# Attention over sorted edges: the running block sum kept in two PSUM banks, copied out by ScalarE at each step, in place of a VectorE add

## The chip, the cores and the metric

The kernel runs on one core of one Trainium2 chip. The metric is the device time of one execution in microseconds (us), as the median of several runs of the same program. All inputs and outputs lie in the chip's memory (HBM).

## The reference

A graph of 6250 nodes (256 values each) and 100000 edges (`src`, `dst`; sorted by `dst`). Two layers are computed, each added to its input: an attention layer with 8 heads of 32 values, then a layer of messages in hyperbolic space. The change touches the attention layer alone:

```
h = relu(layernorm(x));  q, k, v = h @ W + b        # 6250 x 8 x 32 each
scores = sum(q[src] * k[dst]) / sqrt(32)            # 100000 x 8
m = segment_max(scores, dst);  e = exp(scores - m[dst])
z = segment_sum(e, dst);       p = e / max(z[dst], 1e-16)
x = x + segment_sum(v[src] * p, dst)
```

## The kernel before

A first stage sorts the edges for both layers and computes q, k and v. Then comes attention (`attention`), a middle stage, the messages (`messages`) and a last stage. They follow one another and share no work around this change.

In attention the nodes stand in 50 blocks (`NB`) of 127 rows. `acc_l0` in SBUF holds for each block 128 partitions (a node each) x 264 values (`AW`: 8 heads x (32 values and the sum of weights)). The sorted edges go through in 440 steps (`SUPER`) of two groups (`SPAN`) of 128 edges; all edges of a step have their `dst` in one block, whose offset in `acc_l0` is read from a table (`off`) into a register (`Starts.fetch`, L1819, and `Starts.values`, L1822). Four steps (`SG`) make a turn, two turns a window (8 steps, 55 windows). The softmax is taken as a running one: at each window a factor `fac` rescales the block that is being summed.

The code is unrolled: 110 turns, on each engine a function `period(t)` that takes its part of several turns at once (a software pipeline; `old` is four turns back, `ready` three). The engines meet by semaphores alone, and each works strictly in the order that `period` writes.

- TensorE: for each step p of `old`, `sums(old, p)`: two float32 matmuls of the one-hot rows `hot` with the weighted values `pv` into one of two PSUM banks, `out[:, p % 2]` (L2066; each shows as two records); then `near`, two matmuls that pick the keys of a later turn's edges into `kx` (L2046); then in some steps a piece of `chain`, small matmuls for the window's softmax maxima (L2078, L2083, L2087, and L2091 with L2093, which release ScalarE's weights). In a turn's first step `sums` waits for the one-hot rows (`hot_in`), the weights' sums (`z_in`) and the weighed values (`weighed`).
- VectorE: `mult` (L2217), `score` (L2228), `weigh` (L2196), the scans for the maxima (L2247 to L2285), once a window `rescale` (L2206: block times `fac`), and once a step `add` (L2238): block in `acc_l0` = block x `keep` + `out`, where `keep` is 1 if the step before had the same block and else 0. TensorE may refill a bank when its `add` is done (`summed`).
- ScalarE, in a turn: `hot_columns(t+1)` (L2124 after the DMA of marks has landed, L2126), once a window `weights` (L2147, L2150, after TensorE's L2093), `hot_rows(ready)` (eight of L2136, then L2139, which gives `hot_in`), `weight_sums(ready)` (L2158, which gives `z_in`).
- GpSimd gathers the rows of q and v by indirect DMA (L2020); SyncE issues the marks' DMA (L1982) when the second turn back has its keys (`kx_in`).

Of the kernel before, what the change touches and what calls it, by code (L numbers as in the profile page):

```python
# [9 lines left out]
I32 = mybir.dt.int32  # L10
# [1799 lines left out]
class Starts:  # L1810
# [10 lines left out]
    def values(self, first, n):  # L1821
        return [self.eng.snap(r, min_val=0, max_val=self.top) for r in self.regs[first:first + n]]  # L1822
# [66 lines left out]
def attention(nc, m, edges):  # L1889
# [17 lines left out]
    with Stage(nc, "at") as ctx:  # L1907
# [16 lines left out]
        blk, keep = rest[:, 0:1 + SUPER], m.tab_c[:, 2 * SLOT + 2 * G * P + G * DIM:][:, 0:SUPER]  # L1924
# [13 lines left out]
        out = pb("out", [P, 2, 512])  # L1938
# [6 lines left out]
        (c_in, made, hotT_in, hot_in, z_in, kx_in, mixed, scored, weighed, out_in, summed, t1_in, ran, ended, m1_in, carried, m2_in,  # L1945
         came_in, topped, cleared, readied, taken, t2_in, m3_in, far_rows, far_cols, p_in, fac_in, rescaled) = (sem(n) for n in (
             "c_in", "made", "hotT_in", "hot_in", "z_in", "kx_in", "mixed", "scored", "weighed", "out_in", "summed", "t1_in", "ran",
             "ended", "m1_in", "carried", "m2_in", "came_in", "topped", "cleared", "readied", "taken", "t2_in", "m3_in", "far_rows",
             "far_cols", "p_in", "fac_in", "rescaled"))

# [16 lines left out]
        with nc.Block() as block:  # L1967
# [58 lines left out]
            def _(pe):  # L2026
                TE = nc.tensor
                pe.wait_ge(c_in, 32)
                pe.wait_ge(made, 7)
                starts = Starts(pe, "at_pe", off, (NB - 1) * AW, 2)  # L2030

# [18 lines left out]
                def sums(t, p):  # L2050
# [9 lines left out]
                    if p >= 2:  # L2060
                        pe.wait_ge(summed, t.n * SG + p - 1)
                    elif t.plus(-1).exists():
                        pe.wait_ge(summed, t.plus(-1).n * SG + p + 3)
                    for k in range(SPAN):
                        j = SPAN * p + k
                        last = TE.matmul(out[:, p % 2, 0:AW], hot[:, t.h % 2, j, :], pv[:, t.h % 2, j].rearrange("p h d -> p (h d)"),  # L2066
                                         start=(k == 0), stop=(k == SPAN - 1))
# [47 lines left out]
            def _(act):  # L2115
# [3 lines left out]
                def hot_columns(t):  # L2119
# [4 lines left out]
                    A.activation(hotT[:, t.h % 2, :], hotT[:, t.h % 2, :], ACT.Abs, bias=m.minus_lane[:, 0:1]).then_inc(far_cols, 1)  # L2124
                    act.wait_ge(far_cols, t.n + 1)
                    A.activation(hotT[:, t.h % 2, :], hotT[:, t.h % 2, :], ACT.Relu, scale=-1.0, bias=one).then_inc(hotT_in, 1)  # L2126

                def hot_rows(t):
# [3 lines left out]
                    act.wait_ge(col_in[t.h], (t.i + 1) * 16)  # L2132
                    if t.plus(-2).exists():
                        act.wait_ge(out_in, t.plus(-2).n * SG + SG)
                    for k in range(G):
# [5 lines left out]
                def weights(w):  # L2141
# [6 lines left out]
                    if w.plus(-WG).exists():  # L2148
                        act.wait_ge(summed, w.plus(-WG).n * SG + 1)
# [746 lines left out]
```

## Time and profile before

| | |
|---|---|
| median of 3 runs | 3706.06 us (3704.23 to 3707.38) |
| span of the profiled execution | 4137.2 us, 55464 instructions (no time beside the span is given for it) |
| busy in it | PE 73%, PE weight load 58%, DVE 82%, ACT 53%, POOL 48% |
| mean granted TensorE clock | 0.889 of full speed |
| attention in it | from about 764 to 2150 us |

The profiled execution is 431 us longer than the median of the runs that carried no profiler. Engines are called PE, DVE, ACT, POOL and SP in the rows; a trailing q is that engine's sequencer (it issues, waits and loads registers, and is not counted as busy). In a timeline row the numbers are start and duration in us; the brackets hold the time that the engine stood idle before it, and what ended that.

### The profile page before, as it was taken

The page shows a single profiled execution, that of the slowest core. Times are in us where ns is not written, and L with a number is a line of the kernel's source. Part 1 is how long each engine was busy: PE and PEld are TensorE (multiplying, and loading weights), DVE is VectorE, ACT ScalarE, POOL GpSimd, SP SyncE. Part 2 cuts the span into 40 slices and gives each one's busy share as a digit, 9 for nine tenths or more (in the row PEclk, how much of TensorE's full clock was granted, in tenths as well). Part 3 has the DMA queues.
Part 4 walks back from the last instruction along what each step waited for, and adds up shares of the span by engine and source line. Part 5 has one row for each costly group of instructions (what it writes and reads, how often), then busy time and mean ns, then how long its engine had stood idle before and what let it go on. Part 6 is the DMA issues. An engine that isn't in the chain of part 4 may idle for free. (4 is left out here: it accounts for less than half of the span.)

```text
span 4137.2 us, 55464 instructions
## 1 busy us (share of the span) xinstructions
PE 3002.7 (73%) x12662; PEld 2413.6 (58%) x12662; DVE 3401.4 (82%) x9121; ACT 2194.8 (53%) x5961; POOL 1969.1 (48%) x2404
## 2 busy tenths in 40 slices
PE   3545444577777777677756688988988888888866
PEld 2434333455555555555545567777777777777754
DVE  8999996687888888788878378888888888888877
ACT  3235542444444444444438466666665666666557
POOL 1000003556666666666620366666666666666400
PEclk9867777788998889888988899999999999999988
DMA  2111004666667666666636655655655666556361
GB/s 65 39 55 38 13 26 148 191 202 208 202 208 216 207 209 208 211 205 209 206 98 174 172 161 168 173 163 168 171 168 167 167 172 170 166 167 170 89 145 50
DMA packets 295230, 635.60 MB, mean 154 GB/s; under 512 B 78197, under 2 KB 147123, under 8 KB 294657
## 3 DMA queue, kind: packets, MB, share of 16 engines
q0 software_dynamic: 141312, 463.96, 38.3%
q1 hardware_dynamic: 153602, 168.11, 14.5%
q8 instruction: 116, 1.90, 0.2%
q14 instruction: 200, 1.63, 0.1%
HBM read 587.26 MB, written 44.65 MB: 153 GB/s over the span
## 5 line engine op out<-in xcount | busy, mean ns | idle before, releaser
L2469 POOL DMA_INDIRECT area<-d_xr,col x880 | 890.2, 1012 | 686.8 <-DVE area L2706 236.8
L2562 PE MATMUL ms_near_a<-low,ms_hotT 128*128 x1760 | 550.4, 395 | 204.3 <-issue 99.2
L2066 PE MATMUL at_out<-at_pv,at_hot 128*128 128x264 f32 x1760 | 558.6, 447 | 75.7 <-issue 32.0
L2020 POOL DMA_INDIRECT low<-d_qv,col x440 | 449.6, 1022 | 265.6 <-DVE at_pv L2196 129.1
L2563 PE MATMUL ms_near_c<-tab_c,ms_hotT 128*128 x1760 | 536.1, 387 | 0.0
L2046 PE MATMUL at_kx<-area,tab_c 128*128 x1760 | 508.8, 417 | 21.8 <-issue 20.7
L2562 PEld LDWEIGHTS ms_near_a<-low,ms_hotT 128*128 128x128 f32 x1760 | 327.6, 192 | 301.6 <-issue 258.9
L2066 PEld LDWEIGHTS at_out<-at_pv,at_hot 128*128 128x128 f32 x1760 | 358.9, 217 | 161.9 <-issue 63.1
L2046 PEld LDWEIGHTS at_kx<-area,tab_c 128*128 128x128 f32 x1760 | 372.9, 213 | 96.0 <-issue 25.3
L2238 DVE SCALAR_TENSOR_TENSOR area<-area,tab_c,at_out 128x264 f32 x440 | 211.7, 481 | 216.4 <-remote 114.9
L2604 ACT COPY area<-area 128x2 f32<-128x2 f32 x440 | 82.0, 186 | 566.0 <-DVE area L2675 379.0
L2582 PE MATMUL ms_out<-ms_more,ms_hot 128*128 128x257 f32 x1408 | 369.0, 386 | 4.3 <-DVE low L2717 4.3
L2020 POOL DMA_INDIRECT tab_c<-d_qv,col x288 | 294.9, 1024 | 161.6 <-issue 87.2
L2563 PEld LDWEIGHTS ms_near_c<-tab_c,ms_hotT 128*128 128x128 f32 x1760 | 341.0, 194 | 51.6
L2706 DVE CUSTOM_DVE_ANT_0 area<-area 128x256 f32<-128x256 f32 x880 | 342.4, 426 | 23.5 <-issue 12.7
L2672 DVE TENSOR_TENSOR ms_more<-area,ms_near_a 128x514 f32<-128x514 f32 x352 | 239.0, 679 | 140.1 <-PE ms_near_c L2565 73.7
L2124 ACT ACTIVATE tab_c<-tab_c,minus_lane 128x1024 f32<-128x1024 f32 x110 | 126.2, 1147 | 417.8 <-DMA tab_c<-by_dst_marks 374.1
L2582 PEld LDWEIGHTS ms_out<-ms_more,ms_hot 128*128 128x128 f32 x1408 | 272.1, 194 | 47.1 <-ACT ms_more L2640 3.2
L2629 ACT ACTIVATE ms_junk<-ms_more 128x255 bf16<-128x255 f32 x704 | 282.2, 402 | 9.1 <-issue 0.4
L2696 DVE TENSOR_SCALAR ms_hot<-ramp,col,area 128x128 f32<-128x128 f32 x880 | 273.7, 353 | 1.8 <-PE ms_out L2582 1.6
L2136 ACT ACTIVATE at_hot<-ramp,col 128x128 f32<-128x128 f32 x880 | 267.8, 390 | 5.3 <-remote 5.3
L2565 PE MATMUL ms_near_c<-area,ident 128*128 128x256 f32 x880 | 269.1, 388 | 0.0
(375 smaller groups left out, 6560.6 us busy)
## 6 DMA issues: line engine op xcount, KB each, us to landing
tab_c<-by_dst_marks SPq DMA_DIRECT2D x110, 512.0 KB
ms_near_no<-by_src_near SPq DMA_DIRECT2D x110, 224.0 KB
area<-d_xr,col POOLq DMA_INDIRECT x880
d_qv<-low SPq DMA_DIRECT2D x10, 1120.0 KB, 5.0
low<-d_qv,col POOLq DMA_INDIRECT x448
d_xr<-mid_hm SPq DMA_DIRECT2D x5, 1128.8 KB, 6.8
first_x<-in_x_dram SPq DMA_DIRECT2D x5, 1120.0 KB
tab_c<-in_x_dram SPq DMA_DIRECT2D x5, 1120.0 KB, 7.0
```

What stands on the lines that cost most here:

```text
L2020: pool.indirect_dma_start(out=ring[t.n % SLOTS][:, k, :], out_offset=None, in_=m.d_qv, in_offset=bass.IndirectOffsetOnAxis(ap=col[:, t.h, ...
L2046: last = TE.matmul(kx[:, p, k * DIM:(k + 1) * DIM], hotT[:, t.h % 2, (SPAN * p + k) * P:(SPAN * p + k + 1) * P], m.keys[:, bass.ds(at, DIM ...
L2066: last = TE.matmul(out[:, p % 2, 0:AW], hot[:, t.h % 2, j, :], pv[:, t.h % 2, j].rearrange("p h d -> p (h d)"), start=(k == 0), stop=(k == ...
L2136: A.activation(hot[:, t.h % 2, k, :], m.ramp[:, :], ACT.Abs, scale=-1.0, bias=col[:, t.h, k, 1:2].bitcast(F32)).then_inc(far_rows, 1)
L2469: pool.indirect_dma_start(out=far_rows(t, p)[:, k, :], out_offset=None, in_=m.d_xr, in_offset=bass.IndirectOffsetOnAxis(ap=col[:, t.h, SPA ...
L2562: TE.matmul(near_a[:, (SPAN * p + k) % 4, 0:TW], rows, m.tab_a[:, bass.ds(at, TW)], start=True, stop=True)
L2563: last = TE.matmul(near_c[:, p % 2, k * DIM:(k + 1) * DIM], rows, m.tab_c[:, bass.ds(at, DIM)], start=True, stop=p % 2 == 0)
L2565: last = TE.matmul(near_c[:, p % 2, k * DIM:(k + 1) * DIM], m.ident[:, :], far_rows(t, p)[:, k, XB:XW], start=False, stop=True)
L2582: last = TE.matmul(out[:, p % 2, 0:TW], hot[:, j, :], dd[t.slot][:, j, 0:TW], start=(k == 0), stop=(k == SPAN - 1))
L2629: AC.activation(junk[:, k, 1:DIM], dd[t.slot][:, SPAN * p + k, 1:DIM], ACT.Square, accum_out=SQ[:, t.wslot, at:at + 1]).then_inc(squared, 1)
L2696: V.tensor_scalar(hot[:, k, :], m.ramp[:, :], col[:, t.h, k, 1:2].bitcast(F32), cs[:, t.wslot, at:at + 1], ALU.is_equal, ALU.mult).then_in ...
L2706: V.tensor_tensor_reduce(out=row, in0=row, in1=r_aw2, scale=1.0, scalar=0.0, op0=ALU.mult, op1=ALU.add, accum_out=AL[:, t.wslot, k0 + k:k0 ...
```

## The change

The running sum of a block stays in PSUM: blocks with an even number in one bank, with an odd number in the other. Matmuls of a step add onto what the bank holds. `add` and its 440 instructions on VectorE go. In their place:

- ScalarE copies, in every step, the *other* bank (the block before this one) out to `acc_l0` (`keep_block`; a repeated copy writes the same values). TensorE opens a step with two matmuls of zeros with two columns each (`go_on`): one starts accumulation in a bank that gets a new block, one tells ScalarE to copy (`opened`). It waits first until the copy of the step before is done (`kept`).
- In a window's first step the order is: ScalarE copies the running block out (it waits for the last sums of the window before), VectorE rescales it in SBUF, TensorE loads it back into the bank with an identity matmul.
- The offsets of banks and blocks come from two tables made once on VectorE (`work_out_spots`). TensorE reads 8 and 4 entries more a turn into registers, ScalarE 8; VectorE reads 1 a window where it read 4 a turn.
- ScalarE's order: `hot_columns` is cut into `far_columns` and the rest, `hot_rows` into two halves with `keep_block` between the parts, and the weights stand ahead of the rows.

```
 # TensorE, sums(t, p)
-                    if p >= 2:
-                        pe.wait_ge(summed, t.n * SG + p - 1)
-                    elif t.plus(-1).exists():
-                        pe.wait_ge(summed, t.plus(-1).n * SG + p + 3)
+                    go_on(t, p)
+                    at = spots.values(p, 1, OUT_TOP)[0]
...
-                        last = TE.matmul(out[:, p % 2, 0:AW], hot[...], pv[...], start=(k == 0), stop=(k == SPAN - 1))
+                        last = TE.matmul(out[:, bass.ds(at, AW)], hot[...], pv[...], start=False, stop=(ends and k == SPAN - 1))
+                def go_on(t, p):
...
+                    w, j = step_of(t, p)
+                    if p == 0:
...
+                        spots.fetch(t.n * 2 * SG, 2 * SG)
+                        others.fetch(t.n * 2 * SG, SG)
+                    if j == 0:
+                        pe.wait_ge(rescaled, w + 1)
+                        bank, old = spots.values(p, 1, OUT_TOP)[0], spots.values(SG + p, 1)[0]
+                        TE.matmul(out[:, bass.ds(bank, AW)], m.ident[:, :], m.acc_l0[:, bass.ds(old, AW)], start=True, stop=False)
+                        return
...
+                    pe.wait_ge(kept, w * STEPS + j - 1)
+                    TE.matmul(begin, zeros[:, :], zeros[:, 0:2], start=True, stop=False)
+                    TE.matmul(close, zeros[:, :], zeros[:, 0:2], start=False, stop=True).then_inc(opened, 1)
 # ScalarE
+                def keep_block(t, p):
...
+                    if p == 0:
...
+                        spots.fetch(t.n * 2 * SG, 2 * SG)
+                    if j == 0:
...
+                        act.wait_ge(out_in, w * STEPS)
+                    else:
+                        act.wait_ge(opened, w * (STEPS - 1) + j)
+                    if w or j > 1:
+                        act.wait_ge(kept, w * STEPS + j - 1)
+                    A.copy(m.acc_l0[...], out[...]).then_inc(kept, 1)
...
                 def period(t):
-                    hot_columns(t.plus(1))
-                    w = window_before(t)
-                    if w:
-                        weights(w)
-                    hot_rows(t.plus(-LAG))
-                    weight_sums(t.plus(-LAG))
+                    ready, old = t.plus(-LAG), t.plus(-LAG - 1)
+                    far_columns(t.plus(1))
+                    keep_block(old, 0)
+                    hot_columns(t.plus(1))
+                    w = window_before(t)
+                    if w:
+                        weights(w)
+                    keep_block(old, 1)
+                    hot_rows(ready, 0)
+                    keep_block(old, 2)
+                    hot_rows(ready, 1)
+                    keep_block(old, 3)
+                    weight_sums(ready)
 # VectorE
-                def rescale(t, at):
...
-                    V.tensor_tensor(block_at, block_at, bcast(fac[:, :], HD), ALU.mult).then_inc(rescaled, 1)
+                def rescale(t):
...
+                    starts.fetch(t.n * SG, 1)
+                    dve.wait_ge(fac_in, t.window + 1)
+                    if t.window:
+                        dve.wait_ge(kept, t.window * STEPS)
...
+                    V.scalar_tensor_tensor(block, block, keep[:, t.window:t.window + 1], bcast(fac[:, :], HD), ALU.mult, ALU.mult).then_inc(rescaled, 1)
-                def add(t, p, at):
...
-                    V.scalar_tensor_tensor(row, row, keep[:, bass.ds(t.n * SG + p, 1)], out[:, p % 2, 0:AW], ALU.mult, ALU.add).then_inc(summed, 1)
+                    if t.n == 0:
+                        work_out_spots()
```

`work_out_spots` is 13 small instructions on one partition with waits between them, each over up to 440 values, once in VectorE's first turn.

## Rows read from the trace of the kernel before

**Rows 1.** Busy time (us, records) of PE, PEld, DVE, ACT, POOL: attention; messages.
```profile
764.00:2150.00 1386.00, 1010.54 (x3879) 768.12 (x3880) 1125.34 (x2268) 653.91 (x1410) 854.86 (x832) 0.89 0.66 201
...
2331.00:3932.00 1601.00, 1408.60 (x6160) 1180.01 (x6160) 1342.12 (x4842) 1009.83 (x3245) 1037.21 (x1478) 0.97 0.58 164
```

**Rows 2.** The same for one window; last columns: granted clock, DMA share, GB/s.
```profile
1174.08:1198.58 24.50, 16.50 (x73) 12.51 (x73) 20.79 (x43) 12.12 (x26) 17.37 (x17) 1.00 0.72 218
```

**Rows 3.** Timeline of that window: ScalarE and TensorE around a turn's end.
```profile
1174.08 0.28 ACT L2147 ACTIVATE at_pw<-at_ps 128x128 f32<-128x128 f32 x1 [2.86 <-PE at_ps L2093]
...
1174.31 2.44 ACT L2136 ACTIVATE at_hot<-ramp,col 128x128 f32<-128x128 f32 x8
...
1176.78 1.15 ACT L2139 ACTIVATE at_hot<-at_hot,ones 128x1024 f32<-128x1024 f32 x1
...
1177.83 0.29 ACT L2158 COPY at_pv<-at_pw 128x64 f32<-128x64 f32 x1
...
1178.22 1.13 PE L2066 MATMUL at_out<-at_pv,at_hot 128*128 128x264 f32 x4 [0.48 <-ACT at_pv L2158]
```

**Rows 4.** The same timeline, further on.
```profile
1184.01 0.42 DVE L2247 TENSOR_TENSOR_SCAN at_runs<-at_pens,at_pT 128x128 f32<-128x128 f32 x1 [1.37 <-remote]
...
1185.02 0.22 PE L2083 MATMUL at_ps<-at_ends,at_sel 128*8 128x32 f32 x2 [2.85 <-DVE at_ends L2250]
1185.17 1.16 PE L2066 MATMUL at_out<-at_pv,at_hot 128*128 128x264 f32 x4
...
1185.43 0.32 SPq L1982 DMA_DIRECT2D tab_c<-by_dst_marks  x1
...
1187.13 1.05 PE L2066 MATMUL at_out<-at_pv,at_hot 128*128 128x264 f32 x4
1188.02 1.03 PE L2046 MATMUL at_kx<-area,tab_c 128*128 x4
1189.85 0.49 DVE L2238 SCALAR_TENSOR_TENSOR area<-area,tab_c,at_out 128x264 f32 x1 [2.16 <-remote]
1190.26 1.22 DVE L2196 TENSOR_TENSOR at_pv<-tab_c,at_pw 128x1024 f32<-128x1024 f32 x1
...
1191.42 1.15 ACT L2124 ACTIVATE tab_c<-tab_c,minus_lane 128x1024 f32<-128x1024 f32 x1 [7.41 <-DMA tab_c<-by_dst_marks]
...
1191.76 0.40 PE L2087 MATMUL at_ps<-at_carry,at_selT 8*128 8x32 f32 x2 [2.71 <-DVE at_carry L2262]
...
1197.80 0.33 PE L2091 MATMUL at_ps<-ident,low 128*128 128x128 f32 x1 [1.93 <-DVE low L2281]
...
1198.58 0.28 ACT L2147 ACTIVATE at_pw<-at_ps 128x128 f32<-128x128 f32 x1 [4.83 <-PE at_ps L2093]
```

**Rows 5.** Groups by line (busy us, mean ns of one; idle before): the add.
```profile
L2238 DVE SCALAR_TENSOR_TENSOR area<-area,tab_c,at_out 128x264 f32 x440 | 211.7, 481 | 216.4 <-remote 114.9 <-PE at_out L2066 70.6 <-issue 24.8
```

**Rows 6.** Line L1819 in attention (min/median/max ns): loads of 2 and 4 registers.
```profile
L1819 PEldq TENSOR_LOAD <-at_off x211: 516/520/540, 764.6 to 2109.6; - x106
L1819 DVEq TENSOR_LOAD <-at_off x110: 942/946/1174, 763.3 to 2144.6; - x110
```

**Rows 7.** Groups by line that are nearest to new instructions.
```profile
L640 DVE TENSOR_TENSOR sort_kr<-sort_kr 128x448 f32<-128x448 f32 x180 | 112.0, 622 | 3.0
...
L410 ACT COPY area<-qkv_pj 128x256 f32<-128x256 f32 x50 | 18.7, 375 | 7.8 <-PE qkv_pj L320 7.8
...
L1783 PEld LDWEIGHTS fin_p<-fin_bias,fin_ones 128*128 128x128 bf16 x100 | 10.2, 102 | 20.2 <-ACT fin_hT L1695 10.3 <-issue 7.8 <-ACT fin_sT L1695 2.1
```

**Rows 8.** Waits in attention (us in total, times, longest).
```profile
ACT tab_c L2124 <- DMA tab_c<-by_dst_marks: 306.8, 51, 12.1
...
PE at_out L2066 <- ACT at_pv L2158: 28.9, 21, 3.9
```

**Rows 9.** Timeline: TensorE's first record after a stop.
```profile
1731.81 0.81 PE L2066 MATMUL at_out<-at_pv,at_hot 128*128 128x264 f32 x1 [5.14 <-issue]
```

**Rows 10.** Busy time and clock of the 3.4 us behind it.
```profile
1731.80:1735.20 3.40, 3.39 (x8) 2.53 (x8) 3.40 (x9) 0.00 (x0) 0.00 (x0) 0.50 0.01 5
```

More of the change, by code:

```diff
@@ L1819, in fetch, with values @@
         self.eng.load(self.regs[0:n], self.off[0:1, bass.ds(at, n)])
-    def values(self, first, n):
-        return [self.eng.snap(r, min_val=0, max_val=self.top) for r in self.regs[first:first + n]]
+    def values(self, first, n, top=None):
+        return [self.eng.snap(r, min_val=0, max_val=self.top if top is None else top) for r in self.regs[first:first + n]]
     def load(self, at, n):
@@ L1937, in attention @@
         kx = pb("kx", [P, 4, 512])
-        out = pb("out", [P, 2, 512])
+        out = pb("out", [P, 2, 512]).rearrange("p b n -> p (b n)")
+        CLEAR, OUT_TOP = 510, 512
+        zeros = sb("zeros", [P, P], BF16)
         pT = pb("pT", [P, 512])
@@ L2059, in sums @@
                         pe.wait_ge(weighed, 2 * t.n + p // 2 + 1)
-                    if p >= 2:
-                        pe.wait_ge(summed, t.n * SG + p - 1)
-                    elif t.plus(-1).exists():
-                        pe.wait_ge(summed, t.plus(-1).n * SG + p + 3)
+                    go_on(t, p)
+                    at = spots.values(p, 1, OUT_TOP)[0]
+                    ends = step_of(t, p)[1] == STEPS - 1
                     for k in range(SPAN):
                         j = SPAN * p + k
-                        last = TE.matmul(out[:, p % 2, 0:AW], hot[:, t.h % 2, j, :], pv[:, t.h % 2, j].rearrange("p h d -> p (h d)"),
-                                         start=(k == 0), stop=(k == SPAN - 1))
+                        last = TE.matmul(out[:, bass.ds(at, AW)], hot[:, t.h % 2, j, :], pv[:, t.h % 2, j].rearrange("p h d -> p (h d)"),
+                                         start=False, stop=(ends and k == SPAN - 1))
                     last.then_inc(out_in, 1)
@@ L2180, in _ @@
                 V.memset(m.area.rearrange("p (b a) -> p b a", a=AW)[:, :, DIM:AW], 0.0).then_inc(made, 1)
+                V.memset(zeros[:, :], 0.0).then_inc(made, 1)
+                V.memset(out, 0.0).then_inc(made, 1)
                 dve.wait_ge(c_in, 32)
[L2182 to L2184 removed]
+                first_steps = lambda at: blk[:, at:at + SUPER].rearrange("p (w j) -> p w j", j=STEPS)[:, :, 0]
@@ L2289, in period @@
                     ready, old = t.plus(-LAG), t.plus(-LAG - 1)
-                    at = None
-                    if old.exists():
-                        starts.fetch(old.n * SG, SG)
-                        at = starts.values(0, SG)
                     for p in range(SG):
@@ L2296, in period @@
                         if p == 0 and old.exists() and old.h % WG == 0:
-                            rescale(old, at[0])
-                        add(old, p, at)
+                            rescale(old)
                         if p == 0:
```

96 lines of the change are left out of this document (72 added, 24 removed).

## The prediction

> **What bounds the kernel now.** I read busy time by stretch first, because the change touches attention alone. VectorE (DVE) works 1125 of attention's 1386 us [rows 1], 20.5 us in each of the 55 windows, against 16.5 us for TensorE and 12.1 for ScalarE in a window at full clock [rows 2]. So VectorE sets the pace, and it idles 261 us. The timeline says how: in the window of rows 2, two waits of VectorE stand out, 1.37 and 2.16 us, marked "remote" [rows 4]. The second is `add` waiting for sums that started at 1187.13 and should have ended near 1188.2; it starts at 1189.85. Without the two the window would be 24.50 - 3.53 = 21.0 us, which is VectorE's own work. The profiled execution is 431 us longer than the median, and VectorE idles 261 us in attention and 259 in the messages [rows 1]. I put the excess down to such waits, in proportion: 216 us in attention. Then attention takes 1386 - 216 = 1170 us without a profiler, 21.3 us a window. The sum below is a difference against this and goes on the median. If the excess were spread by length, a window would be 1386 * 3706 / 4137 / 55 = 22.6 us; if VectorE never idled, 20.5. These are the ends.
>
> **What is taken away.** 440 adds of 481 ns, 211.7 us of busy time [rows 5], which start some 0.40 us apart (1189.85 to 1190.26 [rows 4]): 8 * 0.40 = 3.2 us a window. `rescale` becomes an instruction of the add's kind and size, 0.48 us [rows 5]. VectorE's loads of 4 table entries, 0.946 us [rows 6], run on its sequencer under a running instruction, so I count nothing. VectorE falls from about 21.0 to 17.8 us a window. It would be the whole gain, 3.2 * 55 = 176 us, if nothing else took its place.
>
> **What is added: prices.** Each is taken from the nearest row.
> - A copy of 264 values out of PSUM: 0.375 us at 256 values [rows 7], so 0.38 us when someone waits for it, 0.30 us when only the next instruction does (spacing of the eight L2136: 2.47 / 8 = 0.31 [rows 3]).
> - A step of TensorE: sums 0.89 (1187.13 to 1188.02 [rows 4]); `near`, with 256 columns for 264, 0.86; so 1.75 us. The identity matmul is half of the sums, 0.45.
> - Two matmuls of zeros: between the 0.15 us that the pair at L2083 takes (1185.02 to 1185.17 [rows 4]) and two loads of bf16 weights plus issue, some 0.25 (0.102 each [rows 7]). I take 0.20, and 0.35 until ScalarE sees the result (between 0.22, L2083's duration, and 0.42, L2091 to L2147 less its second part).
> - Pieces of `chain`: L2083 0.15 us and L2078, one matmul of its kind, as much; L2087 at most its 0.40; from L2091 to ScalarE's L2147 0.78 (1197.80 to 1198.58 [rows 4]).
> - **Register loads.** 2 entries take 0.520 us, 4 take 0.946 [rows 6]: 0.213 an entry and 0.094 beside it. So 8 take 1.80 and 4 take 0.95: TensorE's sequencer needs 2.75 us in each turn for the two new tables. They stand in `go_on`, behind the turn's waits for `z_in` and `weighed`, so they can't start under earlier work that long: what is queued behind them is the whole of the turn's first sums.
>
> The Trainium skill, Runtime: NRT & Kernel Launch, section Instruction fetch mechanics, speaks against such tables: about 200 ns a register even in bulk. By it the 12 entries would take 2.4 us, and the sum below would be lower by 0.35 * 110 = 39 us, an estimate; the traced 0.213 decides.
>
> **The new loop.** Before, ScalarE could be early or late by microseconds without harm (TensorE waited 28.9 us in all for its `z_in` [rows 8]). Now TensorE can't pass a step before ScalarE's copy, and ScalarE can't copy before TensorE has opened the step. I lay out one window, at full clock. *From a turn's first matmul to the opening of its third step.* Even turn (a window's first): identity 0.45, step 1.75, L2078 0.15, zeros 0.20, step 1.75, L2083 0.15, opened 0.35: 4.80 us. Odd turn: two steps with zeros 3.90; L2091 to the weights 0.78, weights 0.23 (L2147 to L2136 [rows 3]), copy 0.38 and 0.05 to answer, because the weights stand ahead of this copy; opened 0.35: 5.69. The third step's copy stands behind half the one-hot rows and starts 0.30 + 1.23 us after the second's, at 6.44 where TensorE has been ready at 5.74: 0.70 more, 6.39 us. *From there to the next turn's first matmul,* in ScalarE's order: answer 0.05, copy 0.30, four rows 1.23, L2139 1.05 (to L2158 [rows 3]), last copy 0.30, L2158 to TensorE's L2066 0.39 [rows 3]: 3.32 us. Then the loads 2.75, and 0.20 for moves and issue: 6.27 us. TensorE has run out of work after 3.95 us of it in an even turn (rest of step 3, step 4, L2087) and 2.85 in an odd one. Ahead of an even turn a second chain runs beside it, L2158 0.29 in place of the 0.39, L2124 1.15 [rows 4], copy 0.38, rescale 0.48, answers 0.10: it ends at 5.33, under the 6.27. A window is 4.80 + 6.39 + 2 * 6.27 = 23.73 us, against 21.27: **+2.46 us, times 55 is +135 us**. VectorE's 17.8 us fit into it; its gain is spent.
>
> **Smaller terms.** `work_out_spots`, 13 instructions of at most 0.62 us (448 values on all partitions [rows 7]), is at most 8 us. It runs in VectorE's first turn, while adds and weighing are not there yet, so between 0 and 8: I take 3. ScalarE's own load of 8 entries, 1.80 us, comes behind L2124's dispatch and under L2139; hidden while the marks have landed. They land 6.0 us after their issue (1185.43 to 1191.42 [rows 4]) and ScalarE waits 306.8 us for them now [rows 8]; in the new loop they are due about when asked for, at worst 2 us late ahead of an odd turn, where the next copy has about 3 us of slack. 0. The clock: after a stop of 5.14 us a matmul took 0.81 us [rows 9] and the next 3.4 us stood at 0.50, the 1.2 GHz level [rows 10]. The mean of 0.89 [rows 1] means 22% of the time at that level, 5.5 us of a window of 25.2, a loss of 2.8 us of TensorE's work. TensorE sets the pace in 10 of the 23.7 us, so between 0 and 1.2 us a window: I take the middle, 0.6 * 55 = 33 us. Sum: 135 + 3 + 33 = 171, and 3706 + 171 = 3877, said as **3880 us**.
>
> **Rivals.**
> 1. *Faster: the loads are hidden.* If TensorE's sequencer reads its tables while queued matmuls run, the odd turn starts at 3.95 (2.32 earlier) and the even one at 5.33 (0.94 earlier): 20.47 us a window, 0.8 under 21.27, so 3706 - 44 + 3 = 3665. For it: two-entry loads cost TensorE nothing visible now. Against: those have no wait ahead of them; these do, and `z_in` comes 3.3 us after the opening when work for only 3.9 is left. It decides from 2.5 of the 3.3 us hidden. Were the copies no hindrance at all, VectorE's 17.8 would be the bound and the time 3520; nothing in rows 3 speaks for that. Chance 17%.
> 2. *No change:* half of the loads hidden, with before's window at 22.6. 3700 to 3713. Chance 5%.
> 3. *Slower still: the clock.* TensorE now stops 3.4 and 2.3 us in each window. If each stop brings a stretch of 3.4 us at 0.50, 1.7 us are lost twice a window: 187 us instead of 33, 4031. For it: rows 9 and 10, though that stop was 5.14 us. Against: in rows 2 waits of 2.85 and 2.71 us left the clock at 1.00. Chance 10%. The Trainium skill, TensorE: Matmul & The Clock Gate, section HAM oscillation — how this bites in real kernels, describes this: a matmul kernel whose bursts are parted by waits starts each burst at half rate.
>
> **How the numbers follow.** The forecast (slower, by the handed-over loop and the loads) has 68%. Its own range is 3740 (before's window at 22.6, nothing for the clock: +63, less 30 for loads partly under the answers) to 3970 (window 20.5: +179; clock 66, spots 8). Rival 3 adds 10%: slower 78%, faster 17%, same 5% (0.2% is about what a measurement of this kernel can tell from no change). The range runs down to 3650, beyond rival 1's 3665, and up to 3990: below it lies under half of rival 1, above it most of rival 3, together near 17%.
>
> **What would show it.** In the changed kernel: L2238's adds gone, VectorE near 920 us busy in attention and waiting for PE or ACT most; two register loads on PE's queue each turn, near 1.8 and 0.95 us, with TensorE idle over them; windows of 24 us or more; ScalarE near 830 us busy; messages unchanged. If loads of eight are much shorter, or TensorE's first sums of a turn start within 0.5 us of L2158, rival 1 holds. If windows stay near 24 but TensorE's records are often at double length, rival 3. It is wrong as a whole if before's windows, unprofiled, were near 24 us.

## The result, and the profile after

| | median us (lowest to highest) |
|---|---|
| before | 3705.14 (3701.55 to 3707.38) |
| after | 4042.61 (4039.16 to 4058.59) |
| ratio | 1.0925, 95% interval 1.0902 to 1.0947 |

The change costs 337 us. Chips differ here: on some the kernel before takes 3705 us, on others about 4142, and the trace behind [rows 1 to 10] was taken on one of the latter, while the times of the table are of the former. So kernels are compared only between chips of one kind below, and each experiment names its chip by what the kernel before took on it.

The same stretches as in [rows 1], first of after, then of the kernel before traced again on a chip where it takes 3705 (its run e11_before):

```profile
744.00:2242.00 1498.00, 1127.30 (x4759) 856.03 (x4760) 967.40 (x1825) 787.60 (x1845) 834.38 (x835) 0.87 0.63 187
2422.00:3830.00 1408.00, 1357.03 (x6146) 1157.79 (x6147) 1331.58 (x4834) 1008.63 (x3245) 1036.34 (x1478) 0.99 0.65 186
```

```profile
743.00:1912.00 1169.00, 953.01 (x3879) 739.49 (x3878) 1117.47 (x2266) 651.49 (x1408) 871.51 (x836) 0.93 0.78 239
2090.00:3498.00 1408.00, 1354.71 (x6136) 1158.32 (x6136) 1329.35 (x4824) 1008.63 (x3245) 1039.37 (x1480) 0.99 0.67 187
```

The messages take 1408 us in both. Attention takes 1498 in place of 1169, so all of the loss lies there: 27.2 us a window against 21.3. VectorE works 150 us less (967 for 1117) and ScalarE 136 us more, and neither is what attention waits for now: even TensorE, the busiest, stands still for 371 of the 1498 us. The granted clock is 0.87 there, which is 2 x 0.13 x 1498 = 390 us at the 0.50 level (1.2 GHz); before it was 0.93, 164 us.

The register loads of after, as in [rows 6] (min/median/max ns; low and tab_c hold the two new tables):

```profile
L1819 PEldq TENSOR_LOAD <-at_off x211: 514/519/541, 743.9 to 2187.1; - x106
L1819 PEldq TENSOR_LOAD <-low x109: 1916/1922/1977, 754.1 to 2233.0; - x109
L1819 PEldq TENSOR_LOAD <-tab_c x109: 980/987/1014, 756.1 to 2235.0; - x109
L1819 ACTq TENSOR_LOAD <-tab_c x109: 1706/1718/1764, 756.5 to 2231.5; - x109
```

TensorE's two take 2.91 us a turn. The new instructions, as groups by line (compare [rows 5, 7]):

```profile
L2100 PE MATMUL at_out<-at_pv,at_hot 128*128 128x264 f32 x1759 | 593.1, 468 | 0.0
...
L2174 ACT COPY area<-at_out x439 | 164.1, 374 | 440.6 <-PE at_out L2065 409.4 <-issue 30.8
...
L2064 PE MATMUL at_out<-at_zeros 128*128 128x2 bf16 x385 | 67.6, 175 | 189.3 <-issue 146.0 <-ACT area L2174 43.3
L2060 PE MATMUL at_out<-area,ident 128*128 x110 | 66.1, 702 | 184.6 <-DVE area L2317 127.0 <-issue 57.6
```

A copy takes 0.374 us, as priced. The identity matmul is TensorE's first instruction after a stop, and its mean of 702 ns is far over the 0.45 us that both of its records should take together. The timeline of one window shows both things, the stop and what follows it (start, duration; in brackets the idle time before and what ended it):

```profile
1508.89 0.39 ACT L2174 COPY area<-at_out  x1
...
1509.42 0.17 PE L2064 MATMUL at_out<-at_zeros 128*128 128x2 bf16 x1 [0.79 <-ACT area L2174]
...
1513.22 0.30 ACT L2224 COPY at_pv<-at_pw 128x64 f32<-128x64 f32 x1
...
1515.50 0.38 ACT L2174 COPY area<-at_out  x1 [0.78 <-issue]
...
1516.09 0.49 DVE L2317 SCALAR_TENSOR_TENSOR area<-area,tab_c,at_fac 128x264 f32 x1 [3.45 <-ACT area L2174]
...
1516.84 1.24 PE L2060 MATMUL at_out<-area,ident 128*128 x2 [3.21 <-DVE area L2317]
1517.87 1.94 PE L2100 MATMUL at_out<-at_pv,at_hot 128*128 128x264 f32 x4
...
1522.76 0.18 PE L2064 MATMUL at_out<-at_zeros 128*128 128x2 bf16 x1
...
1526.64 0.40 PE L2121 MATMUL at_ps<-at_carry,at_selT 8*128 8x32 f32 x2
1529.62 0.17 PE L2064 MATMUL at_out<-at_zeros 128*128 128x2 bf16 x1 [2.58 <-issue]
```

Ahead of the even turn (its identity matmul at 1516.84) TensorE has stood still for 3.21 us, ahead of the odd one (1529.62) for 2.58. The four sums at 1517.87 take 1.94 us where four take 1.05 at full clock [rows 4]. The granted clock (the number after the brackets of POOL) says why: 1.00, then the stop, then 0.55, then 1.00.

```profile
1509.40:1513.00 3.60, 3.58 (x18) 2.91 (x19) 3.21 (x4) 3.57 (x11) 2.99 (x3) 1.00 0.87 288
1513.00:1516.80 3.80, 0.63 (x3) 0.20 (x2) 0.71 (x2) 2.97 (x6) 2.40 (x3) 0.93 0.73 222
1516.80:1520.00 3.20, 3.16 (x8) 2.53 (x9) 0.92 (x1) 0.13 (x1) 1.20 (x2) 0.55 0.28 86
1520.00:1523.60 3.60, 3.60 (x23) 2.79 (x22) 2.64 (x5) 2.05 (x7) 2.59 (x3) 1.00 0.69 184
```

In the whole stage all 55 even turns, each behind a stop of 3.0 us or more, begin with sums at half clock, and so do 25 of the 55 odd turns (stop of 2.6 us in the median; the odd turn of the window shown is one of them). In the trace of after_again it is 55 even and 13 odd turns. Before has some half clock too: its 164 us are 3.0 us a window, where after has 7.1.

### The profile page after: what moved, and what is told of

It reads as the page before. It is cut to its first block and busy times, and to the rows that moved or that the text cites. A ratio compares the mean times of both kernels' runs of the same rounds, so it can differ in the third digit from the quotient of the medians.

```text
span 4037.3 us, 58889 instructions
## 1 busy us (share of the span) xinstructions
PE 3069.2 (76%) x13542; PEld 2481.5 (61%) x13542; DVE 3241.7 (80%) x8696; ACT 2329.6 (58%) x6401; POOL 1944.9 (48%) x2404
## 5 line engine op out<-in xcount | busy, mean ns | idle before, releaser
L2100 PE MATMUL at_out<-at_pv,at_hot 128*128 128x264 f32 x1760 | 593.4, 468 | 0.0
L2660 PE MATMUL ms_near_a<-low,ms_hotT 128*128 x1760 | 535.2, 385 | 64.1 <-issue 40.3
L2031 POOL DMA_INDIRECT low<-d_qv,col x440 | 433.1, 984 | 303.4 <-DVE at_pv L2305 175.7
L2661 PE MATMUL ms_near_c<-tab_c,ms_hotT 128*128 x1760 | 525.5, 380 | 0.0
L2174 ACT COPY area<-at_out x439 | 164.1, 374 | 440.6 <-PE at_out L2065 409.4
L2031 POOL DMA_INDIRECT tab_c<-d_qv,col x288 | 286.1, 994 | 197.7 <-DVE at_pv L2305 118.0
L2200 ACT ACTIVATE at_hot<-ramp,col 128x128 f32<-128x128 f32 x880 | 282.0, 400 | 0.0
L2338 DVE TENSOR_REDUCE at_sc<-tab_c 128x32 f32<-128x1024 f32 x220 | 268.3, 1220 | 7.6
```

What stands on the lines that cost most here:

```text
L2031: pool.indirect_dma_start(out=ring[t.n % SLOTS][:, k, :], out_offset=None, in_=m.d_qv, in_offset=bass.IndirectOffsetOnAxis(ap=col[:, t.h, ...
L2100: last = TE.matmul(out[:, bass.ds(at, AW)], hot[:, t.h % 2, j, :], pv[:, t.h % 2, j].rearrange("p h d -> p (h d)"), start=False, stop=(end ...
L2200: A.activation(hot[:, t.h % 2, k, :], m.ramp[:, :], ACT.Abs, scale=-1.0, bias=col[:, t.h, k, 1:2].bitcast(F32)).then_inc(far_rows, 1)
L2338: V.tensor_reduce(sc[:, k0:k0 + G // 2, :].rearrange("p k h -> p (k h)"), prod[:, k, :].rearrange("p k (h d) -> p (k h) d", d=DH), axis=AX ...
L2660: TE.matmul(near_a[:, (SPAN * p + k) % 4, 0:TW], rows, m.tab_a[:, bass.ds(at, TW)], start=True, stop=True)
L2661: last = TE.matmul(near_c[:, p % 2, k * DIM:(k + 1) * DIM], rows, m.tab_c[:, bass.ds(at, DIM)], start=True, stop=p % 2 == 0)
```

## The experiments

**The two kernels again.** 

before_again, on a chip of 4142:

> The kernel before, once more with a profile, to see attention where the profiled execution is not longer than the others. My account of the stage: 1160 to 1180 us, 21.1 to 21.4 us a window, VectorE idle less than 60 us. If instead attention takes 1240 us or more here, the first profile's waits were the kernel's own and my sum started from the wrong number.

Measured: 4131.77, ratio 0.998 (0.996 to 1.000); attention takes 1386 us there in the trace, as in [rows 1]. So the 431 us between the first trace and the median were the chip's.

after_again, on a chip of 3705:

> The changed kernel, once more, as the measure for the others on the same chip. The chips differ: on the one of the four runs before this the kernel before took 4144 us, with waits of VectorE for TensorE's signals that come late, where it took 3705 us on the first. If such late signals are the chip's, the changed kernel is near 4270 there, with windows above 27.3 us and uneven; on a chip where before takes 3705 it is 4042 again with even windows of 27.3 us.

Measured: 4048.47, ratio 1.093 (1.092 to 1.095). The loss repeats, with windows of 27.4 us.

**The clock.** The edit puts work that is thrown away where TensorE stands still: the key products of the turn's third step are made two or three times, and then once more in their place.

```
+ def fill(t, p, times):           # starts.fetch and the wait for `mixed` as in near
+     for k in [0, 1] * times: TE.matmul(kx[:, p, ...], hotT[...], m.keys[...], start=True, stop=True)
  for p in range(SG):
+     if p == 0: fill(t, 2, 3 if old.h % WG == 0 else 2)
      sums(old, p)
```

e1_fill, on a chip of 4142:

> The changed kernel with TensorE kept busy where it stops: ahead of a turn's waits it repeats the matmuls of the next key product (three times ahead of a window's first turn, twice ahead of the other), same values, nothing else changed. Clock theory: the records at the lower level go or fall below 3 us a window, the window falls from 27.3 to 24 to 25 us, the time from 4042 to 3860 to 3920. Loop theory (loads and hand-over alone are slower than I laid out, the clock is a bystander): the window stays at 27 us or grows by what the added matmuls delay, 4040 or more.

Measured: 4257.94, ratio 1.027 (1.024 to 1.030). The change itself was not run on this chip, so that this says little of what the fill gives back. e8_fill repeated it and fell on such a chip again:

> The changed kernel with the turn's first key products repeated (4 or 6 matmuls more) ahead of TensorE's stops, the kernel of run e1_fill, now beside the kernel before on one chip again. If the half clock (7.2 us a window in the profile after) is what the schedule does not explain, holding TensorE busy through its stops leaves under 3.5 us of it and gives back 1.5 to 3 us a window: 3880 to 3960 us, ratio 1.05 to 1.07. If the clock costs nothing because TensorE is not what the turns wait for, the time stays at 4045 to 4060, ratio 1.093.

Measured: 4273.26, ratio 1.032 (1.028 to 1.036). e12_fill, on a chip of 3705:

> The changed kernel with 4 or 6 repeated key products ahead of each turn's first sums (the kernel of run e1_fill). On a chip where the change takes 4045: if the half clock of 7.2 us a window is what the schedule does not explain, 1.5 to 3 us a window come back, 3880 to 3960 us, ratio 1.05 to 1.07; if the clock costs nothing, 4045 or a little more. On a chip where before takes 4142, again 1.027 to 1.032.

Measured: 3903.97, ratio 1.055 (1.053 to 1.057): 144 us less than after_again, for 1047 more matmul records. The stretch of attention:

```profile
746.00:2102.00 1356.00, 1202.72 (x5806) 943.89 (x5807) 965.03 (x1825) 786.77 (x1845) 841.39 (x833) 0.99 0.69 206
```

The clock is 0.99 where after had 0.87. An even turn begins like this:

```profile
1509.43 2.75 PE L2094 MATMUL at_kx<-area,tab_c 128*128 x12
1512.80 0.71 PE L2060 MATMUL at_out<-area,ident 128*128 x2 [0.62 <-issue]
1513.35 1.05 PE L2112 MATMUL at_out<-at_pv,at_hot 128*128 128x264 f32 x4
...
1517.35 0.18 PE L2064 MATMUL at_out<-at_zeros 128*128 128x2 bf16 x1
```

The four sums take 1.05 us again, and from the identity to the third step's zeros (1517.35) it is 4.55 us, where after had 5.92 in the window shown. The same distances as means over 42 windows, from TensorE's records of both traces, beside what the prediction's loop gives for them (it counted to 0.35 us behind the zeros):

| from, to | predicted | after_again | e12_fill |
|---|---|---|---|
| even turn's start, its third step | 4.45 | 7.24 | 4.59 |
| third step, odd turn's start | 6.62 | 6.88 | 7.11 |
| odd turn's start, its third step | 6.04 | 5.71 | 5.40 |
| third step, next even turn's start | 6.62 | 7.55 | 7.63 |
| window | 23.73 | 27.38 | 24.73 |

The half clock costs about 2.65 us a window, in these 42 windows nearly all in the first two steps of the even turn. The stop ahead of it is the longer one, and the work at half rate there is on the path, since ScalarE, VectorE and the next steps wait for it. It isn't always that one place: where the odd turn begins at half clock too (13 windows of after_again, 24 of after), the even turn's first distance is 6.0 us and the odd turn's 7.0, and the window is 27.3 us again. The 2.65 us are a little too small, if anything: the two distances that hold the thrown-away matmuls are 0.23 and 0.08 us longer with them.

**The register loads.** e2_early reads the tables' entries one by one, three behind each step of the turn before, so that none is left behind a turn's waits:

```
- spots.fetch(t.n * 2 * SG, 2 * SG); others.fetch(t.n * 2 * SG, SG)      # in go_on, p == 0
+ def fetch_next(t, p):                  # called behind near, in each step
+     n = t.plus(1).n * 2 * SG
+     spots.fetch_one(n + p, p); spots.fetch_one(n + SG + p, SG + p); others.fetch_one(n + p, p)
```

On a chip of 4142:

> The changed kernel with TensorE's table entries for the next turn read one by one behind each step (three single loads, some 0.9 us a step, under the running matmuls) in place of 8 and 4 behind the turn's waits. Load theory: a turn's first matmul starts within 0.5 us of ScalarE's L2158 ahead of the odd turn and after the rescale ahead of the even one, 3.3 us a window earlier by my schedule; with shorter stops the lower clock goes as well, in all a window of 20.5 to 22 us, 3670 to 3750. If only the loads matter and the clock stays: 24 us, 3860. If loads were hidden already: 4042.

Measured: 4256.64, ratio 1.026 (1.022 to 1.031); the changed kernel itself has no time on such a chip, so this gives no gain. e16_early, the same on a chip of 3705:

> The changed kernel with the 12 table entries of TensorE's turn read one by one, three behind each step of the turn before, and the order as the change has it (the kernel of run e2_early). On a chip where the change takes 4045: theory of loads as the prediction had it, 2.75 us a turn behind the last wait, but a second chain (ScalarE's copies, rescale) ends 0.94 us earlier than the loads ahead of even turns and 2.3 to 2.75 ahead of odd ones: 3.3 us a window, and less half clock: 3840 to 3890. Rival: it gives no more than the 100 us that lie between e14_near and e6_early_near, 3940 to 3960. On a chip where before takes 4142: again 1.026.

Measured: 3904.53, ratio 1.052 (1.048 to 1.056): 144 us less than after_again, 2.6 us a window. The clock's mean in attention went from 0.87 to 0.93 by itself, so part of the 144 is the half clock's. Under the expected gain, but well over the 100 of its rival. TensorE's waits at the turns' starts, first of after, then of e16_early (us in total, times, longest; L2060 and L2063 are the identity of the even turn, L2064 zeros):

```profile
PE at_out L2064 <- issue: 146.0, 55, 4.5
...
PE at_out L2060 <- DVE area L2317: 127.0, 38, 4.4
...
PE at_out L2060 <- issue: 57.6, 17, 4.6
```

```profile
PE at_out L2063 <- DVE area L2330: 151.6, 54, 3.8
```

Ahead of the odd turns, in after, nothing but issue ended TensorE's wait, which is where its loads run, and in e16_early those stops are gone. Ahead of the even turns the trace of after puts the end of the wait to the rescale in 38 of 55 cases: there the loads end at about the same time as the chain of copy and rescale, and without them TensorE waits for the rescale all the same.

e3_before_loads adds 12 register loads a turn, which nobody uses, to the kernel before, behind its wait for `weighed`; on a chip of 4142:

> The kernel before with TensorE's 12 register loads a turn added at the place where the change has them, their values unused. TensorE has 4.6 us a window without work there, the loads need 5.8: I expect 0.5 to 2 us a window, 3735 to 3815. If register loads run under queued matmuls: 3705 to 3712. If the lower clock follows each stop even here: 3850 or more.

Measured: 4134.36, ratio 0.999 (0.996 to 1.002). This says nothing of the loads, because they are not in the program that ran. Its loads in attention on TensorE's queue are those of the kernel before alone, 211 of two entries, and none of 8 or 4:

```profile
L1819 PEldq TENSOR_LOAD <-at_off x211: 516/520/535, 766.1 to 2102.9; - x106
L1819 PEldq EVENT_SEMAPHORE  x109: 51/51/51, 774.3 to 2138.6; - x109
```

The whole trace has 55464 instructions, as before. So it is the kernel before once more, and what the 12 loads would cost there was not measured.

**The order.** e14_near changes only TensorE's list: the turn's first key products, which need neither weights nor banks, go ahead of its first sums (`near` before `sums(old, 0)`). On a chip of 3705:

> The changed kernel with only the turn's first key products put ahead of its first sums, the register loads as the change has them. With e6_early_near (226 us under the change) it divides that gain. Theory of loads: the loads stand behind the last event that the turn waits for, so the order gives only the 1 us of key products a turn that now run inside the stop, 60 to 110 us, and the loads the rest. Rival, order: the order alone gives 150 to 226 us, since VectorE gets its first product early and the loads run beside it.

Measured: 3922.27, ratio 1.060 (1.058 to 1.061), 126 us less, between what the two theories said. e6_early_near has this and the early loads, on a chip of 3705:

> The same with ScalarE's order left as the change has it: only the early table entries and the key product ahead of the waits. Load and clock theory: at least 200 us under the changed kernel. Order theory (ScalarE's order is what counts): less than half of what the version with both gains.

Measured: 3822.19, ratio 1.031 (1.030 to 1.033), 226 us less. e5_best has ScalarE's list changed beside these two, so that each copy stands where TensorE first wants it:

```
  keep_block(old, 0)          # was behind far_columns
  far_columns(t.plus(1)); hot_columns(t.plus(1))
  keep_block(old, 1)          # was behind weights
  weights(w)
  hot_rows(ready, 0); weight_sums(ready)      # weight_sums was last
  keep_block(old, 2); hot_rows(ready, 1); keep_block(old, 3)
```

> A version meant to keep VectorE's saving: table entries read one by one a turn ahead, the key product of a turn's third step placed ahead of the turn's waits, ScalarE's first copy ahead of the marks, the second ahead of the weights, the weights' sums behind half the rows. If loads, order and the stops that they cause are the cause, a window is 19 to 20.5 us, 60 to 120 us under the kernel before. If the hand-over itself is the bound, it stays above the kernel before.

Measured, on the same chip: 3744.60, ratio 1.011 (1.009 to 1.013): 78 us less again, 304 under the change, and still 40 over before.

e4_no_copies leaves the copies of a window's last seven steps out, with the waits on both sides (finished blocks are not written, so the output is incomplete); the loads and the order are the change's. On a chip of 3705:

> The changed kernel without the copies inside a window: ScalarE copies a block out in a window's first step alone, TensorE waits for no copy in the other seven (finished blocks are lost; the two matmuls of zeros and the register loads stay). What is measured is the price of handing over at each step. By my schedule 0.8 us (the wait behind the weights) and 0.7 (the copy behind the rows) and 0.6 (two copies in ScalarE's tail), 2.1 us a window, 115 us under the changed kernel. If the hand-over is what makes the change slow: 250 us or more under it. If the loads and the clock are all: under 40 us.

Measured: 3972.52, ratio 1.073 (1.071 to 1.075). The copies inside a window cost 76 us, 1.4 a window, less than the 115 expected. Without them the kernel is still 268 us slower than before. That rest isn't the loads and the clock alone: the hand-over in a window's first step (copy, rescale, identity) is still in it, and TensorE waits 224.9 us there for the rescale, in 52 of the 55 windows. How the 268 us divide between the three this run doesn't tell.

**Why the best version doesn't win.** In e5_best VectorE works 966 of 1206 us of attention, TensorE 1054, and GpSimd's waits are all of one kind:

```profile
POOL low L2035 <- issue: 129.2, 424, 0.3
POOL tab_c L2035 <- issue: 82.9, 272, 0.3
POOL at_slot L2035 <- issue: 42.3, 139, 0.3
```

None of its 835 gathers waits for a slot or for VectorE: each starts 0.30 us behind the one before. With 906.86 us of work it is 1.086 + 0.30 us a gather and 22.2 us for the 16 of a window, and the stage's 1206 / 55 is 21.9. Two runs, e9_before_fewer and e10_e5_fewer, were to leave every eighth gather out of the kernel before and of e5_best, but their condition was true in no turn (the loops run when the program is built, and it asked for a turn of a running loop). The traces have as many instructions as those of the kernels that they come from (55464 and 59979). They are repeats, on a chip of 4142:

> The kernel before, with the last of each turn's eight row gathers left out in all turns but the first few (its 128 rows of the slot keep old values, so the output is not the reference's). Theory of gathers: their chain is 2 x 1.32 = 2.6 us a window shorter, and VectorE with its 20.9 us of work becomes the bound at once: 0 to 20 us off the time. If GpSimd alone held the window: up to 140 us off. If VectorE alone does: no change.

> The kernel of run e5_best (the change, with its table entries read one by one, the key products ahead of the turn's first sums and ScalarE's copies at the places where they are due), with the last of each turn's eight gathers left out in all turns but the first few (output not the reference's). In e5_best every gather of the attention stood 0.30 us behind the one before it: 16 x (1.085 + 0.30) = 22.2 us a window of 22.1. Theory of gathers: 14 of them take 19.4 us, so the window falls to 20 to 21 us, where the chain of waits takes over, and the time to 3620 to 3690. Rival (the chain of waits holds it, the gathers just fill the time): the time stays within 15 us of 3745.

Measured: 4147.91, ratio 1.002 (1.000 to 1.004), which shows how near two builds of one kernel come; and 4195.10 for e5_best's kernel, ratio 1.013 (1.011 to 1.016), as on the other chip. e13_e5_fewer leaves them out indeed, on a chip of 3705:

```
+ if k == G - 1 and t.n >= 2 * SLOTS: continue      # GpSimd, in gather_rows
- dve.wait_ge(got[t.n % SLOTS], (t.n // SLOTS + 1) * (16 * G))
+ dve.wait_ge(got[t.n % SLOTS], 16 * (G * uses - max(0, uses - 2)))
```

> The kernel of run e5_best with the last of each turn's eight row gathers left out from turn 12 on, and VectorE's wait lowered to the gathers that are left (those 128 rows of the slot keep old values, so the output is not the reference's). In e5_best every gather of the attention stood 0.30 us behind the one before: 16 x (1.085 + 0.30) = 22.2 us a window of 22.1. Theory of gathers: 14 take 19.4 us, so the window falls to 20 to 21 us, where the chain of waits takes over, and the time from 3745 to 3620 to 3690. Rival (the chain of waits holds it): within 15 us of 3745. On a chip where before takes 4142 gathers are not back to back, and the time stays at 1.013.

Measured: 3628.33, ratio 0.980 (0.978 to 0.982): 116 us less than e5_best. Attention takes 1087 us, 19.8 a window, and the clock rises with it to 0.99:

```profile
745.00:1832.00 1087.00, 1014.78 (x4754) 742.22 (x4755) 960.20 (x1825) 789.58 (x1846) 808.25 (x737) 0.99 0.77 234
```

The gathers were the bound, and with 14 a window they still are: GpSimd's 737 waits in this stretch are all for issue, 226.7 us in all, and 14 x (1.097 + 0.31) = 19.7 us. The chain of waits, which was to take over at 20 to 21 us, was not reached. (The edit takes away the gathers' transfers as well, so it doesn't tell GpSimd's own work from what lies behind it in the DMA queues.) And of the kernel before? e7_before asked for its trace and fell on a chip of 4142 (4137.13 us), so that it says only what the first one does:

> The kernel before once more, for a profile on a chip where it takes 3705 us; the first profile of it was taken on a chip where it takes 4140. Asked: what sets its window of attention (21.1 us by the difference of the two kernels' times) and how long TensorE runs at half the clock in one. Theory of gathers: GpSimd issues the 16 row gathers of a window without a stop, 16 x (1.02 + 0.30) = 21.1 us, gaps of 0.30 us behind nearly all of them. Rival, VectorE: GpSimd waits some us in a window for a free slot, and VectorE is busy for all but 0.3 us of it. On the clock: if the change lost 3.5 us a window to the half clock, before shows under 1 us at half clock in each window, where after shows 7.2; if before shows 5 or more, the clock did not make the difference.

e11_before, on a chip of 3705:

> The kernel before, for a profile on a chip where it takes 3705 us. From the granted clock of its runs there (0.909), less the half-clock time of the other stages (some 510 us in the traces of the changed kernel), its attention should spend 2.9 us of each window at half clock, where the changed kernel spends 7.2. Theory of gathers: nearly all of GpSimd's gathers stand 0.30 us behind the one before, 16 x (1.02 + 0.30) = 21.1 us, the whole window. Rival, VectorE: GpSimd waits 1 us or more of each window for VectorE's at_pv, and VectorE is busy for all but 0.3 us of the window.

Measured: 3712.95 for the one profiled execution. Its waits, GpSimd's and those of VectorE's add:

```profile
POOL low L2020 <- issue: 129.2, 424, 0.3
...
POOL tab_c L2020 <- issue: 82.9, 272, 0.3
...
POOL at_slot L2020 <- issue: 42.6, 140, 0.3
...
DVE area L2238 <- PE at_out L2066: 24.9, 35, 2.1
```

The half clock is 3.0 us a window, for 2.9 expected. Here too every gather is 0.30 us behind the one before, 16 x (1.042 + 0.30) = 21.5 us a window, beside VectorE, which works 1117 of 1169 us. (On the slower chip the add waited 216 us [rows 5] and the gathers 251 us for VectorE, `at_pv`.) e15_before_fewer makes the same cut in the kernel before:

> The kernel before with the last of each turn's eight row gathers left out from turn 12 on (those 128 rows keep old values, so the output is not the reference's). On a chip where before takes 3705, VectorE is busy 20.6 us of a 21.3 us window and the gathers are back to back. If the gathers hold it, the window falls to VectorE's 20.6 and 20 to 40 us go; if VectorE holds it, less than 10 us change. Either way far less than the 116 us that the same edit gave in e13_e5_fewer, since VectorE's adds are still there.

Measured, on a chip of 3705: 3676.41, ratio 0.993 (0.992 to 0.995), 27 us less, and VectorE then works 1115 of 1140 us; GpSimd now waits for it 76 times, 106 us in all. So in the kernel before the gathers come last by a little, and VectorE is right behind them.

## Why the prediction was wrong

The sign was right, and so were the loop of hand-overs and the loads as causes of it. The price of the half clock was far too low, and one chain of the loop was too short. The forecast of 3880 was 163 us too low, and the measured time lies over the range. By the prediction's own steps:

- *Before's window, 21.27 us.* Held: e11_before's attention is 1169 us, where the prediction had 1170. The excess was indeed mostly VectorE's waits (261 us of idle time against 52), but the reason given for it (the profiler) was wrong: it was the chip.
- *What is taken away, 3.2 us of VectorE a window.* Held in size: 150 us less work with the added rescale (967 us of it, not the 920 said under the signs, which took the adds at 0.48 us each and not at their spacing of 0.40). But the step took VectorE for the only bound. Its value could not have been 176 us: with 16 gathers at some 1.34 us the window has a second bound right beside VectorE, and the gathers' price was to be had from [rows 1], 854.86 us for 832 of them, and their 0.30 us of issue. Rival 1's 3665 and its 3520 both lie below what 16 gathers a window allow. Only with fewer gathers did the change's kernel come under before (3628).
- *Prices.* Copy 0.374 for 0.38; loads 1.92 and 0.99 for 1.80 and 0.95; the step, the zeros and the small pieces give 4.59 us from the even turn's start to its third step at full clock, for 4.45. Messages unchanged, as said. The tables (`work_out_spots`), 3 us, can't be told from nothing: attention's first sums start at 743.7 and 742.5 us.
- *The Trainium skill*, Runtime: NRT & Kernel Launch, section Instruction fetch mechanics, has about 200 ns a register even in bulk. The trace has 1.922 / 8 = 0.240 and 0.987 / 4 = 0.247 on TensorE, 0.215 on ScalarE: more, as the row had said.
- *The new loop, 23.73 us.* With the clock held (e12_fill) a window takes 24.73: 1.0 us, 55 in all, was missing. It is missing ahead of the turns' starts, 0.5 us in odd and 1.0 in even ones, and 0.1 in the even turn's first steps, less 0.6 in the odd turn's. One part is seen: ScalarE's load of its 8 entries, costed at 0 ("hidden while the marks have landed"), is not hidden ahead of an even turn. The copy at 1515.50 waits 0.78 us for issue; there are 42 such waits with 30.8 us, and the rescale and TensorE's identity stand behind it. So the second chain, which was to end 0.94 us ahead of TensorE's loads, ends together with them, and in 38 of 55 windows it is what TensorE's wait is put down to. TensorE's two loads take 2.91 us for 2.75, 0.16 more in each turn. That a copy waits for ScalarE's rows is not a missing part: the copies of a turn's last step start 0.9 (even turn) and 1.2 us (odd turn) after TensorE has opened it, in the mean of either trace, and the layout has them behind the rows too. Where the rest of the 1.0 us lies is open.
- *The loads behind the last wait, 2.75 us a turn.* Held ahead of the odd turns: with the loads gone those stops are gone. Ahead of the even turns they are one of two chains that end together. Taking them away gave 144 us, part of it by less half clock. The layout gave 2.32 + 0.94 = 3.3 us a window or 179 us for that; the run has 2.6. So rival 1 was too cheap even without the loads: its 20.47 us were 25 in e16_early. No run shows what such loads cost where no one waits for TensorE.
- ***The clock, 33 us: the step that failed.*** The prediction took 0.6 us a window, the middle of 0 and 1.2, on the ground that TensorE sets the pace in 10 of 23.7 us and that waits of 2.85 and 2.71 us had left the clock at 1.00. Measured: 2.65 us a window, and 144 us given back by filling the stops. The lengths of the stops were not the mistake: by the layout TensorE was to stop 3.4 us ahead of an even turn and 2.3 ahead of an odd one, and it stops 3.3 and 2.6 (means of after). The mistake was to take the waits of 2.85 and 2.71 us as evidence for a stop that the same sum had at 3.4, and to weight the price with TensorE's share of the pace: the half rate falls just on the steps that everybody waits for, so that hardly anything covers it. This is rival 3, which had 10%. It was right in kind and in size less so: it said that both stops bring a stretch and 187 us; the longer one always does, the shorter one in 25 and 13 of 55 windows in two traces, and the price is 146 us. The Trainium skill, TensorE: Matmul & The Clock Gate, section HAM oscillation — how this bites in real kernels, describes bursts that start at half rate after each wait; the 55 of 55 even turns agree, and most of the odd turns, behind the shorter waits, don't.
- *The range.* Its upper end adds up to 3706 + 179 + 66 + 8 = 3959, not 3970, before it is widened to 3990; the measured time lies above either.

Together: 3844 (the sum without its clock) + 55 + 146 = 4045, for 4043 measured. This is an account and not a test, since the 55 and the 146 come from the windows of the same two traces. e12_fill parts the one from the other (to some 0.3 us a window, which its own matmuls may cost); the parts of the 55 that are named are read from traces and were not each tried.

The gains of the single edits do not add up: early loads give 144, the order of key products 126, both together 226. A likely reason, not tried by itself, is that both shorten the same stops and both raise the clock (0.93 and 0.90 in attention, for 0.87).

What stays open: why 684 of the 880 gathers of e11_before take 0.95 us and the others up to 2.0, which is the 0.09 us between their mean and 0.95; and why VectorE hears late of TensorE's sums on the chips of 4142.

## What to carry to other kernels

Before a gain is booked for the busiest engine, look for chains of equal instructions that stand at a fixed distance with only "issue" before them: the gathers with their gaps fill 1126 of attention's 1169 us, beside VectorE's 1117, and left next to nothing of the offered 3.2 us a window from the start. When engines that worked microseconds apart are made to answer one another in each step, whatever stands behind the last wait (a register load of 1.9 us, an instruction of another job in the answering engine's list) is paid for; put it a turn earlier, and look which chain then ends last. And a new stop of TensorE is to be priced with the work that comes after it at half rate when all the others wait for that work: here this was as large as what taking the loads away gave. Three of the edits here (e3_before_loads, e9_before_fewer, e10_e5_fewer) changed nothing in the program that ran: before a run that changes no time is read as "costs nothing", count the new instructions in its trace.

## What the runs showed of the hardware

- Two kinds of chip: the kernel before takes 3705 us on some and 4142 on others. On the latter VectorE is idle for 261 us of attention [rows 1], on the former for 52, and the messages take 1601 us in the first trace, for 1408.
- All 55 even turns, behind stops of 3.0 us and more, begin with work at the 0.50 level in both traces of the changed kernel; of the 55 odd turns, behind about 2.6 us, 25 in the one and 13 in the other. Keeping TensorE busy with useless matmuls through its stops gave back 144 of 4048 us.
- A register load of 8 entries takes 1.92 us on TensorE's queue and 1.72 on ScalarE's, one of 4 0.99, one of 2 0.52.
- A gather by GpSimd of 128 rows takes 0.95 us in 684 of 880 cases and up to 2.0 in the others (e11_before), and the next one starts 0.30 us behind its end when nothing holds it.
